# Edge stage of a message-passing layer: the three filter products of the next super tile wait for the bias copies of their own banks, one by one

## The reference

```python
sj = xs[idx_j];  vj = xv[idx_j]                      # rows of the source nodes
h = shifted_softplus(f_ij @ Wf1 + bf1)               # 40000 x 128
W = (h @ Wf2 + bf2) * rcut_ij[:, None]               # the filters
m_s = s2 * W[:, :2 * F]
m_v = (v2.reshape(e, 2 * F, 3) * W[:, 2 * F:4 * F, None]).reshape(e, 6 * F)
...
agg = jax.ops.segment_sum(x_ij, idx_i, num_segments=n)
```

## Time and profile before

| | |
|---|---|
| time, median of 3 runs | 1503.57 us (1503.35 to 1507.23) |
| the profiled execution's own time | 1502.04 us |
| its span | 1500.3 us |
| PE busy | 1352.4 us (90% of the span) |
| DVE busy | 989.9 us (66%) |
| POOL busy | 755.7 us (50%) |
| ACT busy | 624.4 us (42%) |
| mean granted clock of PE | 0.953 |

### The profile page before, as it was taken

The page is one execution under the profiler, slowest core; times in us unless marked ns, Lnnn a source line. Parts: engine busy times, 40 slices in busy tenths (PEclk is TensorE's granted clock), DMA queues, the critical chain, the costliest instruction groups (busy, mean ns, idle before and its releaser), DMA issues.

```text
span 1500.3 us, 28387 instructions
## 1 busy us (share of the span) xinstructions
PE 1352.4 (90%) x8675; PEld 602.7 (40%) x8676; DVE 989.9 (66%) x2481; ACT 624.4 (42%) x1097; POOL 755.7 (50%) x772
## 2 busy tenths in 40 slices
PE   6557998878869999999999999884999999999997
PEld 4243444434533333333333333372433343433333
DVE  7945666667838777777777777765555565546554
ACT  5454555554525666666666666572111111111110
POOL 4777777777766556665556565604412211211121
PEclk9787999989979999999999999986999999999999
DMA  5665333333249888888888888582352551524513
GB/s 199 227 213 168 114 114 114 111 114 114 97 130 303 251 250 249 251 251 251 250 250 252 250 251 250 160 325 62 72 167 57 192 185 28 196 71 142 193 28 95
DMA packets 125876, 262.54 MB, mean 175 GB/s; under 512 B 21073, under 2 KB 64808, under 8 KB 125147
## 3 DMA queue, kind: packets, MB, share of 16 engines
q0 software_dynamic: 48416, 141.37, 30.8%
q1 hardware_dynamic: 77410, 120.57, 24.3%
HBM read 204.35 MB, written 63.66 MB: 179 GB/s over the span
## 4 chain that ended last, share of the span: by engine, by line
PE 61%; POOL 23%; issue 9%; DVE 4%; DMA 2%; ACT 1%; DVEq 0%; POOLq 0%; SPq 0%; ACTq 0%
POOL edge_list L456 21%; PE psum L1378 19%; PE psum L1873 17%; PE psum L1885 8%; PE psum L1392 7%; PE psum L1387 5%; PE psum L1371 3%; POOL slot_list L1805 1%; DMA out_x<-out_sums 1%; PE psum L1880 1%; DVE msg L1346 1%; DMA slot_list<-pair,slots 0%; PE psum L1576 0%; PE psum L637 0%; ACT aggT L1444 0%
## 5 line engine op out<-in xcount | busy, mean ns | idle before, releaser
L1263 POOL DMA_INDIRECT shared<-node_table,shared x328 | 310.8, 948 | 207.3 <-DVE msg L1344 114.5
L456 POOL DMA_INDIRECT edge_list<-rec,place x313 | 318.1, 1016 | 95.5 <-issue 95.5
L1378 PE MATMUL psum<-wf,hT 128*32 128x512 f32 x2624 | 306.7, 596 | 5.1 <-issue 2.2
L1346 DVE TENSOR_TENSOR msg<-shared,psum 128x768 f32<-128x768 f32 x328 | 310.7, 947 | 0.0
L1873 PE MATMUL psum<-shared,zT 128*64 128x512 f32 (+1 forms) x960 | 295.5, 596 | 1.5 <-DVE zT L1991 1.5
L1301 ACT COPY psum<-bias 128x512 f32<-128x512 f32 x328 | 193.4, 591 | 174.0 <-DVE msg L1346 132.6
L1344 DVE TENSOR_TENSOR msg<-shared,psum 128x256 f32<-128x256 f32 x328 | 136.8, 417 | 129.9 <-PE psum L1378 112.8
L1873 PEld LDWEIGHTS psum<-shared,zT 128*64 128x64 f32 (+1 forms) x960 | 114.1, 159 | 180.5 <-issue 178.6
L1833 POOL DMA_DIRECT2D ids<-slot_list x20 | 11.6, 579 | 289.3 <-DVE zN L1960 266.3
L1885 PE MATMUL psum<-shared,hidT 128*64 128x512 f32 (+1 forms) x480 | 152.7, 596 | 1.5 <-DVE hidT L2012 1.5
L1378 PEld LDWEIGHTS psum<-wf,hT 128*32 128x32 f32 x2624 | 81.1, 110 | 180.2 <-issue 134.4
(11 more groups left out here) (355 smaller groups left out, 1510.9 us busy)
## 6 DMA issues: line engine op xcount, KB each, us to landing
shared<-edge_list SPq DMA_DIRECT2D x332, 130.0 KB
shared<-in_L_ffn_w_gate SPq DMA_DIRECT2D x8, 2048.0 KB, 9.1
shared<-in_L_ffn_w_up SPq DMA_DIRECT2D x8, 2048.0 KB, 14.7
shared<-in_L_ffn_w_down SPq DMA_DIRECT2D x8, 2048.0 KB, 19.4
shared<-node_table,shared POOLq DMA_INDIRECT x328, 3.9
edge_list<-rec,place POOLq DMA_INDIRECT x313, 2.6
raw<-in_records SPq DMA_DIRECT2D x19, 256.0 KB, 3.6
xrow<-in_x SPq DMA_DIRECT2D x10, 250.0 KB
```

Source lines behind the costliest of these rows:

```text
L456: nc.gpsimd.indirect_dma_start(out=edge_list, out_offset=bass.IndirectOffsetOnAxis(ap=place[:n_, c:c + 1].bitcast(U32), axis=0), in_=rec[: ...
L1263: nc.gpsimd.indirect_dma_start(out=gat[:, k % G, :], out_offset=None, in_=table, in_offset=bass.IndirectOffsetOnAxis(ap=ix, axis=0)).then_ ...
L1346: nc.vector.tensor_tensor(m[:, 1:7, :].rearrange("p (a i) f -> p a i f", a=2), g[:, P:D].rearrange("p (i f) -> p i f", i=3).unsqueeze(1).t ...
L1378: ins = nc.tensor.matmul(WP[k % TS][q * W:(q + 1) * W, :], hT[:, (k // TS) % 2, at:at + W], wf2[:], start=False, stop=True, skip_group_che ...
```

## The change

In each super tile PE waited once, ahead of its three products, until all three banks had their bias. Now it waits ahead of each product until that product's own bank has its bias. The last of the three waits is for the same count as the one wait before.

```diff
@@ -1419,8 +1419,8 @@
                                 filters(u * TS + LEAD)
                                 if not last or u + 1 < nu:
                                     pe.wait_ge(h_done, st + 2)
-                                    pe.wait_ge(seeded, st * TS + (TS + LEAD))
                                     for k in range(LEAD):
+                                        pe.wait_ge(seeded, st * TS + (TS + k + 1))
                                         filters((u + 1) * TS + k)
```

## The result

| | before | after |
|---|---|---|
| median of five runs | 1503.57 us (1502.20 to 1507.23) | 1489.92 us (1489.38 to 1492.38) |
| the profiled execution's own time | 1502.04 us | 1492.38 us |
| its span | 1500.3 us | 1490.6 us |

The ratio is 0.9912 with a 95% interval of 0.9898 to 0.9926. The forecast was 1490.8 us, and the range 1488.2 to 1497.2. The change saves 13.65 us by the medians, where 12.8 were forecast. The profiled execution of after happens to be the slowest of its five, so the stage itself must be read from the trace, not from the two spans.

The account below looks back on a forecast made before the run. PE was taken to set the edge stage's pace, busy 507.57 of 512 us. Stops of 11.8 us plus 1.0 at the start, less 0 for added waits, save 12.8: 1503.57 to 1490.8 us, range 1488.2 to 1497.2.

Parts of the forecast that it names:

- The stop and its size: Edge stage, odd super tiles: PE stops for three bias copies together; 26 stops of 0.24 and 13 of 0.43, 11.8 us.
- The cost of the waits: PE's queue, 81 super tiles: 162 added register computations and 162 added waits cost 0 us.
- Rival C: Edge stage on PE: new waits break the flow of weight loads, 0.10 us each; slower, 1507.0 us; chance 0.05.
- What is late next: Edge stage after the change: nothing within PE's reach; DVE still idle some 2.7 us in two super tiles.
- rival A: Edge stage: half the gain comes back as another wait; 6.4 us saved, 1497.2 us; chance 0.07.
- B: Edge stage: DMA of records and gathers sets the pace, so no gain; 1503.6 us; chance 0.04.
- The start: Start of the edge stage, st = 0: the group of three can start some 1.0 us sooner, lower bound 0.
- The sum: Whole kernel: 11.8 + 1.0 - 0 = 12.8 us saved, median 1490.8 us.

Follow-up runs that it names:

- odd only: Changed kernel, but the wait is split in odd super tiles alone, even ones keep the one wait: 1491.78 us, ratio 0.9920.
- even only: Changed kernel, but the wait is split in even super tiles alone, odd ones keep the one wait: 1501.98 us, ratio 0.9987.
- first alone: Changed kernel, but only the first product waits for its own bank; the second waits until the third copy is done: 1492.66 us, ratio 0.9922.
- late copy, one wait: Kernel before, but ACT makes the third copy behind the store of the sums: 1576.86 us, ratio 1.0504.
- late copy with three waits: Changed kernel, but ACT makes the third copy behind the store of the sums: 1488.36 us, ratio 0.9923.
- last first: Changed kernel, but the first of the three waits is for the third copy, so nothing is freed: 1502.71 us, ratio 1.0010.
- twelve waits: Changed kernel, but the wait is repeated ahead of each of the group's twelve matmuls: 1488.77 us, ratio 0.9926.
- waits only: Kernel before with its one wait kept and the three new waits added behind it: 1505.40 us, ratio 1.0012.
- after again: The changed kernel timed once more, nothing altered: 1489.91 us, ratio 0.9919.
- records early: Changed kernel, but SP issues the records of st = 3 and 4 without waiting for the first three gathers: 1487.73 us, ratio 0.9900.

## Why the prediction was right

**The stop and its size.** Right. The forecast for the steady stage was 11.8 us, from 26 stops of 0.24 and 13 of 0.43; it gave 11.75. That they lie in odd super tiles is shown by odd only and even only, that the first product's wait is the cause by first alone, and that the copy's lateness is what PE pays for by the two late copies.

**The cost of the waits.** Right, and more firmly than argued: waits that are already satisfied cost nothing that the steady stage can show, two a super tile with their register computations (last first) or twelve (twelve waits). Rival C is out. What one row of DVE's queue gave, 0.10 us a wait, doesn't hold for PE while its array is fed. The Trainium skill gives 50 to 100 ns for reading a semaphore from a sequencer (Advanced Engine Details and Errata, section Network/Comms). On PE nothing of that size shows, except where PE is stopped already: the doubled wait of waits only cost 0.077 us a stop. That this is such a read is not shown.

**What is late next.** Right for the steady stage, and a little too generous in size. I counted the slack of the copies, 2.4, 2.1 and 1.7 us, up to the products' start in the chain. PE's loads stand earlier: 1.8, 1.5 and 1.1 us behind the copies by the timeline after. But a load can be 0.40 us late before time is lost (last section), so a copy could come about 2.2, 1.9 and 1.5 us later. In the steady stage no other wait came into the place of the one removed, so rival A is out there; so is B, since the stage shortened by what was freed while the DMA share only rose to 0.84. In st = 1 of the first profile after, a small piece of A did come: the third product's own copy was late.

**The start.** The term of 1.0 us is borne out in size, but it wasn't safe. From tile 3's load to the first of st = 2 it took 13.15, 13.25, 13.71 and 13.13 us where st = 0 had the one wait (before, waits only, odd only, last first). With all three waits split in st = 0 and st = 1 it took 12.15, 12.29 and 12.15 (twelve waits, late copy with three waits, after again), and 12.23 in records early. So four of the five profiles with the full split are 0.8 to 1.6 us below those with the one wait. The fifth is the first profile after, 13.40, where the late copy and the late records took the lead back. The prediction said that PE and DVE waited for a transfer but once, for 0.28 us. The first turn and the first message had waited for transfers too, for 6.2 and 16.5 us, and the statement left out what would be late once PE came sooner. Neither first alone nor even only tests the term: one keeps a wait for the third copy in st = 0, the other a wait for all three in st = 1.

**The sum.** 12.8 forecast; 13.65 by the medians. The interval of the ratio allows 11.1 to 15.3 us. The difference of 0.9 lies inside that. That the medians came so near is in part luck: the median of before alone moved by 2.3 us from one group of runs to another. For the profiled execution I had forecast 1489.2 us and a span of 1487.5, and both came out 3.1 to 3.2 too small. The stage gave 12.0 of the 12.8 in that execution (11.75 steady, 0.24 at the start), and what follows the products of st = 80 took 543.7 us in place of 541.6, which belongs to the scatter above.

## What to carry to other kernels

When one wait stands ahead of several pieces of work with separate inputs, look at the piece in front: if its input is early and the last input is late by less than the pieces in between take, the stop goes away by waiting for each alone, and the waits are free where the engine is kept fed. Judge by the weight loads and by pieces of the chain, not by busy time: PE was 99% busy by the windows with 11.75 us of stops in it, mostly hidden as pieces that took 2.78 in place of 2.57 us. And put the measure inside the stage, from one repeated instruction to another: it repeated to 0.01 us where whole executions scatter by several.

## What the runs showed of the hardware that was not expected

PE's weight loads can come about 0.40 us late before anything is lost. The table sets the idle ahead of the late load, less the usual 0.30, against the time lost in that super tile, its products against 3.43.

| where | idle ahead of load | later than usual | lost | difference |
|---|---|---|---|---|
| before, st = 1 | 0.71 | 0.41 | 0.01 | 0.40 |
| before, ordinary odd | 0.94 | 0.64 | 0.24 | 0.40 |
| before, behind the start of a pass | 1.13 | 0.83 | 0.43 | 0.40 |
| waits only, ordinary odd | 1.01 | 0.71 | 0.32 | 0.39 |
| late copy, one wait, mean of 78 | 1.77 | 1.47 | 1.07 | 0.40 |

The loads of the first and third row, from the timeline of before:

```profile
460.29 0.16 PEld L1378 LDWEIGHTS psum<-wf,hT 128*32 128x32 f32 x8 [0.71 <-ACT psum L1301]
...
763.53 0.16 PEld L1378 LDWEIGHTS psum<-wf,hT 128*32 128x32 f32 x8 [1.13 <-issue]
```

So st = 1 of before had a late load as well, and lost nothing since it was late by no more than 0.41 us. The 1.07 of the last row is 83.6 us over 78 super tiles; the idle there is 1.76 us in most and 1.83 in one of six. What is lost is the lateness of the load less 0.40, about the time of one set of matmuls at the pace of one set each 0.43 us. That the set already loaded covers the time is my reading of it; no run took it apart.
